# Post-norm attention and ternary feed-forward on one core: the engines' orders redrawn, block 0's normalisation split between GpSimd and VectorE, dummy products left out

## What is computed

```python
# attention; q, k, v = x @ Wq, x @ Wk, x @ Wv in 16 heads of 8; fg = sigmoid(x @ Wf + bf)
state = state * gt[..., None] + vt[..., None] * kt[..., None, :]
out_t = jnp.einsum('bhij,bhj->bhi', state, qt)
...
out = (out - mu) * jax.lax.rsqrt(var + EPS) * gamma + beta
out = out * jax.nn.silu(x @ Wg)
return out @ Wout
# feed-forward; _tlin(x, w, s) = einsum('bsi,oi->bso', x, w) * s
h = jax.nn.silu(_tlin(x, w1_w, w1_s)) * _tlin(x, w2_w, w2_s)
h = jax.nn.gelu(_tlin(h, h1_w, h1_s), approximate=False)
h = jax.nn.gelu(_tlin(h, h2_w, h2_s), approximate=False)
return _tlin(h, w3_w, w3_s)
# whole: x = layernorm(x + attention(x)); x = layernorm(x + feed_forward(x))
```

## Time and profile before

| what | value |
|---|---|
| median of 3 runs | 507.65 us (507.61, 507.65, 510.7) |
| span of the profiled execution | 505.3 us |
| around the span, taken against the median | 2.3 us |
| TensorE, VectorE, ScalarE, GpSimd busy | 98%, 89%, 80%, 61% |
| granted TensorE clock, mean | 1.000 |

### The profile page before, as it was taken

How to read it: one execution, slowest core, us unless ns; L and a number is a source line. 1 busy time by engine, 2 the same in 40 slices (tenths; PEclk the granted TensorE clock), 3 DMA queues, 4 the chain that set the end, 5 groups by cost and what they waited for, 6 DMA issues and landing times.

```text
span 505.3 us, 8095 instructions
## 1 busy us (share of the span) xinstructions
PE 495.5 (98%) x2528; PEld 383.7 (76%) x2528; DVE 447.2 (89%) x708; ACT 405.6 (80%) x839; POOL 310.0 (61%) x362
## 2 busy tenths in 40 slices
PE   8999999999999999999999999999999999999997
PEld 6667787877878787777877777787777778687896
DVE  4999899999999999999999999899999999994171
ACT  5677788887897877879798787989878797978955
POOL 0842839577392948748394875748486584928423
PEclk9999999999999999999999999999999999999999
DMA  7999989718079976698897790880797592520001
GB/s 257 226 252 240 208 215 221 194 48 205 0 187 227 244 180 134 155 219 197 190 237 180 178 236 3 189 208 1 169 225 168 138 210 71 121 67 1 22 3 65
DMA packets 43372, 79.47 MB, mean 157 GB/s; under 512 B 4928, under 2 KB 5952, under 8 KB 43072
## 3 DMA queue, kind: packets, MB, share of 16 engines
q1 hardware_dynamic: 43040, 78.61, 63.7%
q10 hardware_dynamic: 288, 0.33, 0.2%
HBM read 11.81 MB, written 4.19 MB: 32 GB/s over the span
## 4 chain that ended last, share of the span: by engine, by line
PE 69%; DVE 9%; issue 8%; POOL 8%; ACT 3%; SPq 2%; DMA 1%; POOLq 0%; ACTq 0%; DVEq 0%
PE F L2301 41%; PE back L2402 8%; PE front L2202 6%; DVE KJ L1557 4%; PE back L2287 2%; POOL h1lo L441 2%; PE back L2186 2%; PE ps_v L2202 2%; POOL h2lo L441 2%; PE back L2269 2%; SPq L283 2%; POOL KJ L502 1%; PE F L2198 1%; DMA QJ<-qk 1%; DVE h L1621 1%
## 5 line engine op out<-in xcount | busy, mean ns | idle before, releaser
L441 POOL TENSOR_TENSOR h1lo<-h,h1hi 128x512 fp32r<-128x512 f32 x60 | 76.4, 1290 | 18.5 <-ACT h1hi L864 18.2
L871 ACT ACTIVATE h<-F,cols 128x512 f32<-128x512 f32 x120 | 80.5, 686 | 8.6 <-PE F L2301 7.6
L441 POOL TENSOR_TENSOR h2lo<-h,h2hi 128x512 fp32r<-128x512 f32 x60 | 76.1, 1290 | 10.6 <-ACT h2hi L864 10.4
L1557 DVE TENSOR_TENSOR_SCAN KJ<-g,carry,KJ 128x512 f32<-128x512 f32 x64 | 78.3, 1264 | 0.3 <-ACT g L803 0.2
L1557 DVE TENSOR_TENSOR_SCAN KJ<-g,KJ 128x512 f32<-128x512 f32 x64 | 74.3, 1203 | 0.4 <-ACT g L803 0.3
L508 POOL TENSOR_TENSOR QJ<-QJ 128x512 f32<-128x512 f32 x14 | 18.0, 1283 | 91.6 <-DVE QJ L1572 91.6
L2301 PE MATMUL F<-h2hi,whi 128*128 128x512 f32 (+1 forms) x256 | 72.1, 417 | 0.7 <-ACT h L871 0.5
L1564 DVE TENSOR_TENSOR QJ<-QJ,KJ 128x1024 f32<-128x1024 f32 x60 | 71.4, 1213 | 1.0 <-DMA QJ<-qk 0.8
L2301 PE MATMUL F<-h1hi,whi 128*128 128x512 f32 (+1 forms) x256 | 70.7, 414 | 1.0 <-DVE h L1621 0.8
L2301 PE MATMUL F<-h1lo,whi 128*128 128x512 f32 (+1 forms) x256 | 67.7, 401 | 0.2 <-POOL h1lo L441 0.2
L2301 PE MATMUL F<-h2lo,whi 128*128 128x512 f32 (+1 forms) x256 | 66.4, 402 | 0.0
(11 more groups left out here) (182 smaller groups left out, 937.9 us busy)
## 6 DMA issues: line engine op xcount, KB each, us to landing
KJ<-qk SPq DMA_DIRECT2D x120, 256.0 KB, 4.8
QJ<-qk SPq DMA_DIRECT2D x120, 256.0 KB, 4.8
x_in<-in_x SPq DMA_DIRECT2D x16, 256.0 KB, 4.7
xT<-in_xT SPq DMA_DIRECT2D x15, 256.0 KB, 5.0
out<-res SPq DMA_DIRECT2D x15, 256.0 KB, 2.0
wraw<-in_wffn SPq DMA_DIRECT2D x2, 1024.0 KB, 8.8
wraw<-in_wffn SPq DMA_DIRECT2D x2, 256.0 KB, 4.7
wproj<-in_wproj SPq DMA_DIRECT2D x2, 192.0 KB, 3.7
```

The lines of the kernel that those rows point to most:

```text
L441: e.tensor_tensor(h_lo[layer][:, t, :w], h[:, t, :w], h_hi[layer][:, t, :w].bitcast(f32), ALU.subtract).then_inc(lo_done[layer], 1)
L871: e.activation(dst[:, t, :WIDTH[n]], F[t][:, :WIDTH[n]], ACT.Gelu, scale=scale[t]).then_inc(gelu_done[layer], 1)
L1557: e.tensor_tensor_scan(K, g[:, :WIDTH[n]], K, init, ALU.mult, ALU.add).then_inc(scan_done, 1)
```

## The change

Three things change. `keep_busy` and its five calls go. In block 0 GpSimd makes only the two powers (`power_of`); VectorE makes the sum with epsilon (`spread_of`) and the shift (`shift_of`), and the semaphores that follow them are chosen by `gated` and `mv_free`. And the lists of calls of all five engines are redrawn from block 0 to the tail. The halves of a fetch may now come in either order, so each half carries its waits.

```diff
@@ block 0's norms
+    NORMS_DVE, GATES_DVE = range(0, 1), range(0, 1)
+            def power_of(n, k):
+                r = rstd[k][:, n % 2, :len(chunks(n))]
+                e.wait_ge(ve_done[k], n + 1)
+                e.tensor_tensor(r, r, mhalf4[:, :len(chunks(n))], ALU.pow).then_inc(rstd_done[k], 1)
...
+            def spread_of(n, k):
+                nc_ = len(chunks(n))
+                e.wait_ge(mv_done[k], n + 1)
+                e.tensor_scalar(rstd[k][:, n % 2, :nc_], mv[k][:, :nc_, 1], EPS, None, ALU.add).then_inc(ve_done[k], 1)
+
+            def shift_of(n, k):
+                nc_ = len(chunks(n))
+                e.wait_ge(rstd_done[k], n + 1)
+                e.scalar_tensor_tensor(shift[k][:, n % 2, :nc_], mv[k][:, :nc_, 0], -1.0, rstd[k][:, n % 2, :nc_],
+                                       ALU.mult, ALU.mult).then_inc(shift_done[k], 1)
@@ GpSimd, start
             kvj_gp(4)
+            kvj_gp(6)
             qsj_gp(1)
-            kvj_gp(6)
             qsj_gp(2)
-            scale_w3()
             qsj_gp(3)
             kv_gp(1, 4)
             kv_gp(1, 5)
-            rstd_of(0, "o")
             kv_gp(1, 6)
             kv_gp(1, 7)
-            rstd_of(0, "1")
+            power_of(0, 'o')
+            power_of(0, '1')
@@ VectorE, start
             scan(0, 0)
+            scan(0, 1)
             kvj(3)
-            scan(0, 1)
             kvj(5)
...
             kv(1, 0)
+            kv(1, 1)
             qsj(7)
             scan(1, 0)
+            scan(1, 1)
             stats_o(0)
-            kv(1, 1)
-            scan(1, 1)
-            half_norm("o")
+            spread_of(0, 'o')
             scan(1, 2)
+            shift_of(0, 'o')
+            half_norm('o')
             scan(1, 3)
-            gated_y0()
             scan(1, 4)
+            gated_y(0)
+            qs(1, 0)
             residual_1(0)
-            qs(1, 0)
+            find_low_parts()
             stats_1(0)
+            spread_of(0, '1')
             scan(1, 5)
+            shift_of(0, '1')
+            set_flag()
+            half_norm('1')
             scan(1, 6)
-            half_norm("1")
-            find_low_parts()
+            scan(1, 7)
+            x1_lo(0)
             qs(1, 1)
-            set_flag()
-            x1_lo(0)
-            scan(1, 7)
             qs(1, 2)
@@ ScalarE, start
+            copy_v(0)
             hi_0(0)
             hi_0(1)
-            copy_v(0)
...
+            copy_qj(3)
+            sum_low_parts(0)
             copy_kj(6)
-            sum_low_parts(0)
-            copy_qj(3)
             tanh(1)
+            sum_low_parts(1)
+            copy_k(2)
             copy_v(1)
-            copy_k(2)
+            sum_low_parts(2)
+            split_weights(0)
             g_of_tanh(1)
@@ TensorE, around the branch
             project_gate(0)
-            keep_busy(4, back)
             project_gate(1)
-            keep_busy(1, back)
+            transpose_y(0)
+            project_k(3)
+            attention_out(0)
             project_v(2)
-            project_k(3)
-            transpose_y(0)
+            count_low_parts()
             project_q(2)
-            attention_out(0)
-            keep_busy(10, F[3])
-            keep_busy(16, F[3])
-            transpose_x1(0)
-            count_low_parts()
-            keep_busy(1, F[3])
             project_gate(2)
...
             def rest(low_parts):
+                transpose_x1(0)
+                project_q(3)
                 up_hi(0, 0, low_parts)
                 up_hi(0, 1, low_parts)
                 up_lo(0, 0, low_parts)
                 up_lo(0, 1, low_parts)
-                project_q(3)
+                project_k(4)
@@ GpSimd, one block as an example: the norm behind the low parts
             lo(2, 7, 2)
-            rstd_of(7, "1")
             lo(2, 7, 3)
+            rstd_of(7, '1')
+            rstd_2(5)
@@ VectorE, block 15: residual_1(14) two scans later
             scan(15, 3)
+            scan(15, 4)
+            scan(15, 5)
             residual_1(14)
-            scan(15, 4)
             stats_1(14)
-            scan(15, 5)
@@ the tail: TensorE and ScalarE
-                last_block(0)
-                last_block(1)
                 tail_hi_products(2, 1, 3, low_parts)
...
                 tail_lo_products(2, 1, 3, low_parts)
+                last_block(0)
+                last_block(1)
                 last_block(2)
                 last_block(3)
...
             tail_gelu(2, 1, 2)
+            norm_2(13)
             tail_gelu(2, 1, 3)
+            norm_2(14)
```

More of the change, by code:

```diff
@@ L117, in kv_pairs @@
         def kv_pairs(n):
-            return sum(2 if m in EARLY else 3 for m in range(1, n))
+            return sum(2 if m in KV_HALF else 3 for m in range(1, n))
         def kv_gpsimd(n):
-            return sum(4 if m in EARLY else 2 for m in range(1, n))
+            return sum(4 if m in KV_HALF else 2 for m in range(1, n))
         def adds_gpsimd(n):
@@ L1699, in _ @@
             scan(0, 3)
+            scan(0, 4)
             kvj(7)
-            scan(0, 4)
             scan(0, 5)
@@ L1745, in _ @@
             scan(2, 4)
+            scan(2, 5)
             residual_1(1)
             stats_1(1)
-            scan(2, 5)
             scan(2, 6)
             scan(2, 7)
+            qs(2, 0)
             qs(2, 1)
+            qs(2, 2)
+            x1_lo(1)
             add(2, 0)
-            x1_lo(1)
-            qs(2, 2)
             qs(2, 3)
@@ L1785, in _ @@
             hmul(2, 0)
+            hmul(2, 1)
             residual_2(1)
-            hmul(2, 1)
             kv(4, 0)
@@ L1835, in _ @@
             add(5, 0)
+            add(5, 1)
             qs(5, 3)
-            add(5, 1)
             add(5, 2)
@@ L1860, in _ @@
             x1_lo(5)
+            add(6, 0)
             qs(6, 2)
-            add(6, 0)
             qs(6, 3)
@@ L1865, in _ @@
             add(6, 2)
+            hmul(5, 0)
             residual_2(4)
[L1867 removed]
             hmul(5, 1)
@@ L1884, in _ @@
             scan(7, 7)
-            x1_lo(6)
             qs(7, 0)
@@ L1888, in _ @@
             qs(7, 2)
+            x1_lo(6)
             add(7, 0)
+            add(7, 1)
             qs(7, 3)
-            add(7, 1)
             add(7, 2)
@@ L1983, in _ @@
             kv(11, 1)
+            scan(11, 0)
+            kv(11, 2)
+            scan(11, 1)
+            qs(11, 0)
             scan(11, 2)
             scan(11, 3)
-            kv(11, 2)
-            qs(11, 0)
-            qs(11, 1)
             scan(11, 4)
+            scan(11, 5)
             residual_1(10)
             stats_1(10)
-            scan(11, 5)
             scan(11, 6)
             scan(11, 7)
+            qs(11, 1)
             qs(11, 2)
+            x1_lo(10)
             add(11, 0)
-            x1_lo(10)
+            add(11, 1)
             qs(11, 3)
-            add(11, 1)
             add(11, 2)
-            kv(12, 0)
             hmul(10, 0)
@@ L2004, in _ @@
             residual_2(9)
-            scan(12, 0)
+            kv(12, 0)
             hmul(10, 2)
@@ L2023, in _ @@
             x1_lo(11)
+            scan(12, 7)
             add(12, 0)
@@ L2042, in _ @@
             scan(13, 4)
-            scan(13, 5)
             residual_1(12)
             stats_1(12)
+            scan(13, 5)
             scan(13, 6)
             scan(13, 7)
+            qs(13, 0)
             qs(13, 1)
             qs(13, 2)
+            x1_lo(12)
             add(13, 0)
-            x1_lo(12)
             add(13, 1)
@@ L2193, in warm_up @@
                     e.matmul(F[0][:, :P], y[:, :P], y[:, :P], start=True, stop=True)
-            def keep_busy(products, bank):
-                for k in range(products):
-                    e.matmul(bank[:, :P], ident[:], WV, start=True, stop=True)
             def project(n, bank, weights):
+                if n == 0:
+                    e.wait_ge(wproj_landed[0], 16)
                 e.wait_ge(xT_landed[n % XTB], 16 * (n // XTB + 1))
```

1074 lines of the change are left out of this document (530 added, 544 removed).

## The result

The changed kernel took 514.11 us (median of 4 runs, 513.09 to 514.41), the kernel before, run beside it, 508.82 (4 runs, 507.61 to 510.7): ratio 1.0102, 95% interval 1.0071 to 1.0134. Forecast were 507.1 us, "within 1%", and a range that ended at 512.5. The profiled execution spans 512.2 us, 6.9 more than the one before.

What follows compares the result with a forecast made beforehand. TensorE was taken to bound blocks 1 to 11, VectorE the last four. From 507.65 us, -0.35 (block 0's start), 0 (body) and -0.2 (tail) gave 507.1 us; range 502 to 512.5.

Steps and rivals of the forecast that it cites:

- What bounds the kernel: Whole kernel: TensorE bounds blocks 1 to 11, VectorE the last four; TensorE loses 12 us to waits after the start.
- Part 3, the body: Redrawn orders of blocks 1 to 15: no operation added or removed, costed at 0, bounds -6 to +6 us.
- the body loses: Rival, blocks 1 to 15: residual_1 one or two scans later makes TensorE wait; +5 to +6, 513 us; chance 0.12.
- Part 1, the dummies: Block 0: removing dummy products returns nothing by itself; projections done in the wait leave TensorE 0.86 us less to do.
- The rival: Clock rival, block 0 into the first FFN: without dummies TensorE's clock falls to half rate; 510 us; chance 0.12.
- Part 2, block 0's chain: First scan to block 1's sum: sum starts 0.5 us later with 0.86 less to do, -0.35 us, bounds -1.7 to +3.
- the branch: Block 0, now ahead of the transposes of x1: 1.15 us from the flag's end to the first product behind it.
- Part 4, the tail: Last block: two of four output products move to the end, -0.2 us, bounds -0.5 to +1.0.

Runs made afterwards that it cites:

- e1: The changed kernel with GpSimd's four short operations of block 2's norm of x1 ahead of layer 2's last low part, not behind it: 510.73 us, ratio 1.0019.
- f3: The kernel before with its 32 dummy products in block 0 left out, nothing else changed: 511.27 us, ratio 1.0068.
- g1: The kernel before with the changed kernel's order at one place, block 2's norm of x1 and VectorE's steps around it: 513.34 us, ratio 1.0088.
- g2: The kernel before's start and tail with the changed kernel's orders between, block 2's norm of x1 ahead of the low part: 506.82 us, ratio 0.998.
- g3: The kernel before with the changed kernel's tail orders on TensorE, VectorE, ScalarE and GpSimd: 509.71 us, ratio 1.0022.
- e3: The changed kernel with powers and final scalings of blocks 13 and 14, and so their stores, where the kernel before has them: 513.63 us, ratio 1.0097.
- e4: The changed kernel with the kernel before's whole tail orders on TensorE, VectorE, ScalarE and GpSimd: 511.23 us, ratio 1.0051.

## Why the prediction was wrong, point by point

**What bounds the kernel: right.** No run contradicts the busy shares and the price of TensorE's stream; between blocks 3 and 15 all profiles of the changed orders agree within 0.3 us.

**Part 3, the body: the step that failed.** I wrote of GpSimd's short operations "none is held for long, and a plan that reserves time for holds buys slack that isn't used". I had looked at where the kernel before places them (while VectorE scans, all at 0.20) and read it as a property of the operations. It was a property of the place: in the kernel before none of the four ever starts inside a run of VectorE's products with q, and the change moved one there. The Trainium skill has the rule that I didn't weigh (GPSIMD Engine Reference, 1. Specifications: GpSimd shares its SBUF interfaces with VectorE and contends with instructions that have two SBUF inputs). This trace agrees on both sides. The products with q read QJ and KJ, both in SBUF, and each one of 128x1024 in the run holds for 1.2 us, three at worst. VectorE's scans read g and its products `kv` read `ps_v`, both PSUM banks, and in the changed kernel the short operations that fall inside them, 58 in scans and 18 in `kv`, take 0.19 to 0.22. One such place cost 3.0 to 3.4 us (e1): the hold itself, TensorE's wait, and 3 us at half clock behind it. My rival "the body loses" named a later residual and up to 513 us; its place was right (block 3 is one where the residual moved), its mechanism wasn't.

**Part 1, the dummies: wrong.** "Their removal returns nothing by itself" is true, and it left out that it takes something: 3.3 us if nothing replaces them (f3). With projections in the hole it takes 1.0 us of that stretch in three of five executions, and nothing in the changed kernel's own profile. The rival priced this at 510 and 2.4 to 2.9 us. Its mechanism was right; its size was 1.0 with the changed start, and in f3 1.9 of the 3.3 lie in the stretch that I priced. What I took for its weakness ("no hole is as long as the 6 us") wasn't one: in e1 the clock fell behind a hole of 1.94 us.

**Part 2, block 0's chain: right up to the branch, which was mis-sized.** From the first scan to the residual I forecast 37.2 - 10.4 = 26.8 us; it took 38.04 - 11.12 = 26.9. The first scan came 0.7 later than forecast: there the executions differ by themselves (9.8 to 11.3 in the nine profiles with that start; 10.4 in the profile before, but 10.9 to 11.3 in its four relatives g1, g2, g3, f3). So 0.7 of the 1.8 us at the start were the good start of the one profile that I had. For the branch I took 1.15 us from the flag's end to the first product behind it, in the changed kernel it was 43.66 - 41.61 = 2.05, and up to 2.5 in the others.

**Part 4, the tail: wrong.** The products did what I said: from block 15's output product to TensorE's end 37.4 us, 37.6 before, so -0.2. But I costed nothing behind the last operation, where a moved step can act through the DMAs: the norms of blocks 13 and 14 carry their 256 KB stores, and I costed the norm (1.3) and not the store. The tail's orders as a whole are worth +1.5 us (g3) to +2.4 (the two traces), behind the last operation. That the two stores do it isn't shown: with them back in their old places e3 still has 3.6 us there.

**The range.** Its upper end, 512.5, came from one cause at a time. Three of them came together: 3.4 + 1.5 + 2.2 us, less 1 for the body. And the 5 us that I held for the least that a measurement can tell were too many: the intervals here reach 0.2 to 0.4% either way.

## What to carry to other kernels

Before moving a short operation of GpSimd, look at what VectorE runs at its new place. Beside back-to-back products whose two operands lie in SBUF it lasts one product or the whole run here. If an engine's next input hangs on it, everything behind waits, and one line swapped in GpSimd's queue is then worth more than the whole redrawing; if nobody waits for it, the hold is free. Filler work of an engine is to be costed by a run without it, and by the granted clock in that run's windows, not by asking whether its time was free. And a profile of one execution has its own luck: compare stretches (scan to residual, last product to end), and take the relatives' spread before giving a term a tenth.

## What was not expected of the hardware

- The same local order, with the short operation starting 0.03 to 0.04 us ahead of VectorE's first product each time, gave a hold of 1.30 us in one execution (e3) and 3.57, 3.56 and 3.56 in three others (the changed kernel, e4, g1).
- A 128x512 GpSimd operation in progress slows VectorE's product instead (two products 2.87 us instead of 2.33, e1), where a 128x4 one is itself held.
- In the first microseconds the passes of a projection stood 0.85 us apart in some executions and 0.43 in others, while the granted clock read 1.00 in both. The changed kernel, and below it e3:

```profile
4.62 1.91 PE L2225 MATMUL ps_v<-xT,wproj 128*128 128x512 f32 x2
```

```profile
4.39 1.10 PE L2225 MATMUL ps_v<-xT,wproj 128*128 128x512 f32 x2
```

Between these two it is 1.1 of the 1.3 us by which their first scans differ. No run here tried to change it.
